# Order sums of a polynomial attention layer as accumulating transfers, and a reordered vector queue

## The reference

```
h = _layernorm(x) * (1 + ca) + sa
x = x + ga * attn(h, W_in, W_out)
h = _layernorm(x) * (1 + cb) + sb
x = x + gb * ffn(h, ...)

# attn, per head of 16 channels
Tq, Tk = cheb(clip(q / 4)), cheb(clip(k / 4))
kv_beta = cumsum(Tk * v, axis=sequence) * beta
k_beta = cumsum(Tk.sum(channels), axis=sequence) * beta
num = (Tq * kv_beta).sum(orders)
den = (Tq.sum(channels) * k_beta).sum(orders)
out = (num / (den + 1e-7)) @ W_out.T

# ffn: top 2 of 8 experts, weight sqrt(softplus(logit)), plus the shared expert
y = shared(h) + sum_e combine[e] * (silu(h @ rW1[e] + rb1[e]) @ rW2[e] + rb2[e])
```

## Time and profile before

| | us |
|---|---|
| median of 3 runs (1147.56, 1149.32, 1340.12) | 1149.32 |
| the profiled execution's own time | 1148.21 |
| its span, first to last instruction | 1146.2 |

### The profile page before, as it was taken

One profiled execution on the slowest core, in us unless ns is written; L12 is line 12 of the kernel. 1 busy time (PEld: TensorE's weight loads), 2 busy tenths in 40 slices (PEclk: granted clock), 3 DMA queues, 4 the chain that ended last, 5 costly groups with the idle time before them and its releaser, 6 DMA issues.

```text
span 1146.2 us, 15452 instructions
## 1 busy us (share of the span) xinstructions
PE 968.0 (84%) x4889; PEld 689.4 (60%) x4889; DVE 962.7 (84%) x1465; ACT 521.1 (45%) x755; POOL 440.3 (38%) x606
## 2 busy tenths in 40 slices
PE   4865569898989899898989899898989899787997
PEld 3634255666757576666757476666757576555775
DVE  1499789989898998989898998989899898889542
ACT  4433344454536454454535455454635445342331
POOL 2044242443625254443525244443525243343220
PEclk9776779999999999999999999898989999888999
DMA  7100000000101010000101000010100000000000
GB/s 256 43 1 18 1 28 1 19 19 1 47 1 37 1 43 4 14 23 0 47 0 37 0 33 13 2 35 0 47 0 19 0 20 9 0 19 1 23 19 19
DMA packets 23069, 25.79 MB, mean 23 GB/s; under 512 B 1043, under 2 KB 21982, under 8 KB 23014
## 3 DMA queue, kind: packets, MB, share of 16 engines
q1 hardware_dynamic: 21410, 22.72, 6.1%
q10 hardware_dynamic: 1604, 2.46, 0.7%
HBM read 16.77 MB, written 8.40 MB: 22 GB/s over the span
## 4 chain that ended last, share of the span: by engine, by line
DVE 40%; PE 29%; issue 19%; POOL 4%; ACT 3%; DVEq 1%; POOLq 0%; ACTq 0%
PE ring L1256 14%; DVE feat L934 11%; PE acc L1390 11%; DVE feat L900 3%; DVE feat L902 3%; DVE hidL L1095 2%; DVE feat L957 2%; POOL feat L628 2%; DVE hid L1090 2%; DVE feat L891 2%; PE cfb L1364 1%; PE tr L1339 1%; DVE feat L992 1%; DVE feat L953 1%; DVE best L1065 1%
## 5 line engine op out<-in xcount | busy, mean ns | idle before, releaser
L765 ACT ACTIVATE hid<-ring,b1row 128x512 f32<-128x512 f32 x144 | 98.2, 686 | 175.4 <-PE ring L1256 175.1
L1390 PE MATMUL acc<-w,hid 128*128 128x256 f32 x640 | 155.4, 390 | 0.0
L1256 PE MATMUL ring<-n2H,w1H 128*128 128x512 f32 x288 | 106.1, 451 | 56.5 <-ACT feat L723 56.5
L1090 DVE TENSOR_TENSOR hid<-hid,cfb 128x512 f32<-128x512 f32 x128 | 86.6, 676 | 80.1 <-PE cfb L1364 79.7
L1390 PEld LDWEIGHTS acc<-w,hid 128*128 128x128 f32 x640 | 116.4, 190 | 27.9 <-issue 14.7
L636 POOL TENSOR_TENSOR best<-best,pool_c 128x8 f32<-128x8 f32 x16 | 27.1, 1693 | 257.2 <-DVE best L1071 257.2
L628 POOL TENSOR_TENSOR feat<-feat 128x1024 f32<-128x1024 f32 x32 | 96.6, 3036 | 9.2 <-DVE feat L953 6.9
L673 POOL TENSOR_TENSOR fin<-fin,x 128x512 f32<-128x512 f32 x32 | 52.9, 1673 | 117.0 <-DVE fin L1104 117.0
L934 DVE TENSOR_TENSOR_SCAN feat<-zero,carry,feat 128x512 f32<-128x512 f32 x80 | 97.1, 1265 | 0.0
L1256 PE MATMUL ring<-n2H,w1L 128*128 128x512 f32 x288 | 96.9, 419 | 0.0
L1256 PE MATMUL ring<-n2L,w1H 128*128 128x512 f32 x288 | 96.7, 419 | 0.0
(11 more groups left out here) (169 smaller groups left out, 2253.4 us busy)
## 6 DMA issues: line engine op xcount, KB each, us to landing
xin<-in_L_attn_x SPq DMA_DIRECT2D x16, 512.0 KB, 3.6
out<-fin SPq DMA_DIRECT2D x16, 512.0 KB, 2.9
gates<-gate_rows SPq DMA_DIRECT2D x16, 128.0 KB, 3.5
feat<-in_L_wmod SPq DMA_DIRECT2D x1, 1536.0 KB, 13.8
feat<-in_L_attn_W_in SPq DMA_DIRECT2D x1, 768.0 KB, 9.2
const<-in_constants ACTq DMA_DIRECT2D x1, 690.5 KB, 4.3
fin<-in_constants ACTq DMA_DIRECT2D x1, 512.0 KB, 5.4
w<-in_L_ffn_rW ACTq DMA_DIRECT2D x1, 512.0 KB, 8.9
```

The source lines that it names most:

```text
L765: a.activation(hid[:, e % NG], ring[bank][:, :], ACT.Silu, bias=b1row[:, e:e + 1]).then_inc(ring_copied, 1)
L1090: v.tensor_tensor(hid[:, e % NG], hid[:, e % NG], cfb[:, :], ALU.mult).then_inc(hidw_ready, 1)
L1256: last = mm(out, w, x, start=(n == 0), stop=(n == len(terms) - 1))
L1390: last = mm(acc[t // 2][:, t % 2], x[:, t * P:(t + 1) * P], w[:, e // 2], start=False, stop=(e == E), skip_group_check=True)
```

## The change

- Three of the four sums of the order products are now DMA transfers with an add, issued from POOL: orders 1 into 0, 3 into 4, then 4 into 0. DVE adds order 2 at the end. Two POOL instructions of 128x1024 and one of DVE go.
- DVE's calls are reordered: each `prefix` is followed soon by its product, order 2 is weighed and summed last, the statistics of chunk c+2 stand behind the third prefix sum, `odd` of the query stands behind the residual, and the carry is copied for each order apart.
- The gate `ga` is multiplied into W_out once per batch row on POOL (`scale_wo`), not into the projection's result on DVE.
- The residual x1 goes to the output by a plain store of SP, and the gated expert output is added to it in memory by a transfer from POOL, in place of two POOL additions and a store.
- The exponential of the routing is a power on POOL, not an activation on ACT.
- The tile `split` is half as wide, and three of its four transposes are smaller.

```diff
+        wo_g = sb("wo_g", [P, KD, D])
...
-            def store(i, p):
-                sp.wait_ge(fin_ready, 2 * number(i, p) + 2)
-                sp.dma_start(o_v[i, p], fin[:, :, :]).then_inc(stored[p], 16)
+            def store_x1(i, p):
+                sp.wait_ge(x1_ready, 2 * number(i, p) + 2)
+                sp.dma_start(o_v[i, p], x1[:, p]).then_inc(x1_stored[p], 16)
...
-            def add_orders(i, p):
+            def add_orders(i, p, n):
                 c = number(i, p)
-                for n in range(2):
+                if n < 2:
                     pool.wait_ge(products, ND * c + 2 * n + 2)
-                    g.tensor_tensor(f(W + 2 * n), f(W + 2 * n), f(W + 2 * n + 1), ALU.add).then_inc(added, 1)
+                else:
+                    pool.wait_ge(added[0], 16 * c + 16)
+                    pool.wait_ge(added[1], 16 * c + 16)
+                into, of = ((W, W + 1), (W + 4, W + 3), (W, W + 4))[n]
+                pool.sem_inc(sum_begun, 1)
+                g.dma_start(f(into), f(of), accum_op=ALU.add).then_inc(added[n], 16)
+
+            def exps(i, p):
+                c = number(i, p)
+                pool.wait_ge(log_parts, NLOG * c + 4)
+                ge(pool, soft_steps, NSOFT * c)
+                g.tensor_tensor(best[:, U].rearrange("p t k -> p (t k)"), k_("e", NT * K),
+                                best[:, NEG].rearrange("p t k -> p (t k)"), ALU.pow).then_inc(exp_ready, 1)
...
-            def add_residual(i, p):
-                c = number(i, p)
-                for h in range(2):
-                    pool.wait_ge(ffn_gated, 2 * c + h + 1)
-                    o = fin[:, 2 * h:2 * h + 2]
-                    g.tensor_tensor(o, o, x1[:, p, 2 * h:2 * h + 2], ALU.add).then_inc(fin_ready, 1)
+            def add_to_output(i, p):
+                pool.wait_ge(x1_stored[p], 16 * (i + 1))
+                pool.wait_ge(ffn_gated, 2 * number(i, p) + 2)
+                g.dma_start(o_v[i, p], fin[:, :, :], accum_op=ALU.add).then_inc(stored[p], 16)
+
+            def scale_wo(i):
+                pool.wait_ge(gate_loaded[0], 16 * (i + 1))
+                ge(pool, projected, 2 * number(i, 0))
+                ga = gates[:, 0:1].to_broadcast([P, KD, D])
+                g.tensor_tensor(wo_g[:, :, :], wo[:, :, :], ga, ALU.mult).then_inc(wo_ready, 1)
...
                 silu(5)
                 high(4)
                 copy("v0")
...
-            ORDERS = (0, 1, 3, 2, 4)
+            ORDERS = (0, 1, 3, 4, 2)
+            BY_WEIGHT = (0, 1, 3, 2)
...
             def finish_numerator(i, p):
                 dve.wait_ge(products, ND * c + ND)
-                dve.wait_ge(added, 2 * c + 1)
-                v.tensor_tensor(f(W), f(W), f(W + 4), ALU.add).then_inc(numerator, 1)
-                dve.wait_ge(numerator, 2 * c + 1)
-                dve.wait_ge(added, 2 * c + 2)
+                dve.wait_ge(added[2], 16 * c + 16)
                 v.tensor_tensor(f(W), f(W), f(W + 2), ALU.add).then_inc(numerator, 1)
...
             def residual(i, p):
-                dve.wait_ge(gate_loaded[0], 16 * (i + 1))
+                ge(dve, x1_stored[p], 16 * i)
                 for h in range(2):
                     dve.wait_ge(projected, 2 * c + h + 1)
-                    v.tensor_tensor(gated[:, h], tr[h][:, :].rearrange("p (t d) -> p t d", t=2), gate(0),
-                                    ALU.mult).then_inc(gated_ready, 1)
-                ge(dve, fin_ready, 2 * c - 2)
-                for h in range(2):
-                    dve.wait_ge(gated_ready, 2 * c + h + 1)
-                    v.tensor_tensor(x1[:, p, 2 * h:2 * h + 2], gated[:, h], xin_of(i, p)[:, 2 * h:2 * h + 2],
-                                    ALU.add).then_inc(x1_ready, 1)
+                    v.tensor_tensor(x1[:, p, 2 * h:2 * h + 2], tr[h][:, :].rearrange("p (t d) -> p t d", t=2),
+                                    xin_of(i, p)[:, 2 * h:2 * h + 2], ALU.add).then_inc(x1_ready, 1)
```

More of the change, by code:

```diff
@@ L3 @@
 from contextlib import ExitStack
+import math
 import numpy as np
@@ L111, in build @@
         tie = cv["tie"].unsqueeze(1).to_broadcast([P, NT, E * E])
-        PC = ("-half", "half", "one", "eps", "1/D")
+        PC = ("-half", "half", "one", "eps", "1/D", "e")
         pool_c = sb("pool_c", [P, len(PC)])
@@ L219, in build @@
         x_loaded = [sem(f"x_loaded{p}") for p in range(CB)]
+        x1_stored = [sem(f"x1_stored{p}") for p in range(CB)]
         stored = [sem(f"stored{p}") for p in range(CB)]
@@ L238, in build @@
         products = sem("order_products")
-        added = sem("orders_added")
+        added = [sem(f"orders_added{n}") for n in range(3)]
+        sum_begun = sem("order_sums_begun")
         numerator = sem("numerator")
@@ L431, in _ @@
                 for n, what in enumerate(PC):
-                    value = {"-half": -0.5, "half": 0.5, "one": 1.0, "eps": EPS_LN, "1/D": 1.0 / D}[what]
+                    value = {"-half": -0.5, "half": 0.5, "one": 1.0, "eps": EPS_LN, "1/D": 1.0 / D, "e": math.e}[what]
                     nc.gpsimd.memset(pool_c[:, n:n + 1], value).then_inc(s_pow, 1)
@@ L601, in _ @@
                 step(0, p, False, True)
-            with sp.Fori(1, B - 2) as i:
+            for p in range(CB):
+                step(1, p, True, True)
+            with sp.Fori(2, B - 2) as i:
                 for p in range(CB):
@@ L1120, in step @@
                     residual(*prev)
-                if second:
                     token_stats(dve, 1, *prev)
+                if attn_:
+                    odd(i, p, 1)
                 low(0)
@@ L1145, in step @@
                     prefix(i, p, 2)
-                if qkv:
-                    clip(*nxt, use, 0)
-                    clip(*nxt, use, 1)
+                if norm:
+                    token_stats(dve, 0, *after2)
+                if attn_:
+                    order_product(i, p, 2)
+                    prefix(i, p, 3)
+                expert(4)
+                if attn_:
+                    order_product(i, p, 3)
+                low(4)
                 if second:
@@ L1214, in _ @@
                 clip(0, 0, CHUNK0, q)
-            for q in range(2):
-                odd(0, 0, q)
+            odd(0, 0, 0)
             for i, p, st in FIRST:
@@ L1350, in combine_by_expert @@
                     pe.wait_ge(log_parts, NLOG * c + 1)
-                for t in range(NT):
-                    last = nc.tensor.transpose(misc[:, t * P:(t + 1) * P], split[:, t], ident)
+                nc.tensor.transpose(misc[:, 0:P], split[:, 0:2].rearrange("p t j -> p (t j)"), ident)
+                for t in range(1, NT):
+                    last = nc.tensor.transpose(misc[0:P // 2, t * P:(t + 1) * P], split[:, t], ident)
                 last.then_inc(split_T, 1)
```

118 lines of the change are left out of this document (55 added, 63 removed).

## The result

| | median us | of the kernel before |
|---|---|---|
| before | 1149.24 (4 runs) | 1 |
| after | 1179.16 (1178.51 to 1179.65, 4 runs) | 1.0265, 95% interval 1.0245 to 1.0285 |

The kernel got slower by 30 us. The profiled execution of the kernel after took 1179.41 us, with a span of 1177.7.

The account below looks back on a forecast made before the run. The prediction took a step as a ring paced by PE, DVE, then PE: 16.3 + 27.15 + 22.35 = 65.8 us against 64.7. Twelve steps add 13, the edges take 10: 1148.2 became 1151, range 1105 to 1190.

Parts of the forecast that it names:

- The chain: From DVE's late statistics over POOL's inverse roots, ACT and DVE to the v0 copy: sets the pace, 1137 to 1166, 0.55.
- the edges: Steps outside the twelve: two first -1.5 each, last first half -3, the one behind -3, last two -1; together -10.
- rival 2: Third transfer of the sums lands late, finish_numerator waits: each of 14 steps 3.2 us longer, total 1196; chance 0.12.
- Stretch A: Step start to the spread of expert 2, PE sets the pace: 16.6 us before, 16.3 after, transposes' 1.11 wait gone.
- Stretch B: Spread of expert 2 to the v0 copy and e6, DVE sets the pace: 23.9 us before, 27.15 after.
- term I: Time of POOL's inv_std for the first norm, between 4.9 and 7.3 us by the rows; taken as 6.1.
- Stretch C: From e6 to the next step's start, PE sets the pace: 23.6 us before, 22.35 after, two short waits gone.
- The sum: One step: 16.3 + 27.15 + 22.35 = 65.8 us against 64.7, +1.1; over twelve steps +13 us.
- The transfers: Accumulating transfers issued on POOL: 5.8 us landing and 1 us issue, 6.8 within 10.4 of slack, so no cost.
- Rival 3: POOL isn't freed, descriptors take as long as the additions, 3.04 us each; total stays 1151; included in the forecast's 0.55.
- Rival 1: Statistics don't limit, POOL hardly held, ACT early: step 63.0, total 1118, or 1099 without ACT's wait; chance 0.25.
- What would show it: Signs in the changed profile: steps 65 to 67 us, hidden_low idle 3 to 5, e6 gap 6 to 7, landing 5 to 8.

Follow-up runs that it names:

- e6: Not a run: expert 6 of the step, whose expert_up on PE waits for ACT's copy of v0.
- e4: Not a run: expert 4 of the step, whose hidden_low on DVE waits for its high part from ACT.
- the first experiment: Kernel after with one edit on DVE: the first norm's token statistics right behind the weighting of expert 2, ahead of the scans of prefix 1 and 2; 1154.98 us.
- two edits: On the kernel after with normalise_first late: last weighting of values ahead of hidden_low of expert 4, 1118.04 us; with the denominators' inverse ahead too, 1065.20 us.

## Why the prediction was right and wrong

The mechanism was right, its size was not: 1151 forecast, 1179 measured. The likeliest outcome named was no change that can be measured (0.47, against 0.26 for slower); it is 2.65% slower. The chain as I had summed it reached from 1137 to 1166 and a few us more for the edges, and 1179 lies above that. It lies inside the range of 1105 to 1190 only because the range had been widened upwards for rival 2, which did not occur; that part is luck. By the steps of the prediction, in the step from 567.87:

- **Stretch A**, 16.3 forecast. `weigh_hidden` of expert 2 starts at 584.12, 16.25 behind the start. The sum is right, its split is not: PE reached the spread after 14.96, earlier than the 15.5 that I took (16.6 - 1.1), and DVE started 1.3 behind it instead of 0.8 (the hand-over and the charge of 0.4 each), with its two scans at 4.5 us beside POOL's weighting. The wait at the transposes is gone, as forecast.
- **Stretch B**, 27.15 forecast, 29.46 measured (584.12 to 613.58). Here lies most of the miss, in the size of the terms and not in the chain: every link stands in the trace in the order that I gave. DVE up to the end of the statistics 12.0 (11.3): I had left out the small carry copies of 0.17 us that now follow each pair of scans in the step of a first half, and the start gap of 0.23 at 594.73. The term I, from there to ACT's start, 7.26 (6.1). ACT 3.20 (3.3). DVE from `hidden_low` to the end of the `weigh` 6.0 (5.7). From there to e6 0.97 (0.75).
- **The term I** is 1.16 of these 2.31 us. I took the middle of 4.9 and 7.3; the row to take was that of 7.3, since a product and scans stand back to back beside it in the new place. Four of its twelve instructions took 1.05 to 1.16 us in place of 0.2. That is 3.6 us of holds on the 3.3 of the unhindered twelve. With 7.3 in the sum, though, the forecast is 67.0 for a step, still 1.2 short of the measured 68.2.
- **Stretch C**, 22.35 forecast, 23.03 measured. The waits of 0.41 and 0.84 are gone. "PE is cold behind its gap as before, at no new cost" is the sentence that fell: PE waited twice, 8.9 us in all, and the clock behind was 0.50 where it had been 0.61. From e6 to the matmul of the head sums (613.58 to 619.30) PE took 5.7 us where it had taken 5.0 (590.50 to 595.50), and that is the 0.7 by which C is over.
- **The sum.** 68.74 in this step and 67.72 in the next, against 65.8. The excess of 2.4 us on average, twelve times, is 29 us, and the forecast lacked 28. The edges came to -11 for a forecast of -10, but term by term that is luck: the stretch ahead of the twelve steps is 3.6 us shorter (3 forecast), the two steps behind them 5.5 and 7.2 (3 each), and all that follows 5.1 us longer (1 shorter). Nearly all of the last is the end of the run: from DVE's last product to the last instruction, 5.4 us before and 9.9 now that a transfer that adds ends it. I had written "nothing either way" there.
- **The transfers**, 6.8 us for issue and landing forecast. Issue 0.92, landing 4.6. The third was issued at 616.89 and `finish_numerator` began at 628.45 without a wait: 11.6 us for 5.5. Rival 2 did not occur. Only in the two first steps, which have no experts, did `finish_numerator` wait for a transfer, 3.66 and 1.22 us, as the forecast had it. The Trainium skill, "DMA: Bandwidth & Descriptors", section "Anatomy of one DMA — SWDGE (gpsimd) path", gave 3.2 us by estimate; the trace has 4.6 for the transfers that add.
- **Rival 3**, POOL not freed, did not occur: an issue is 0.92 us of POOL, an addition 2.4 to 3.0. POOL's busy time in all stayed at 441 us even so, for it also has the exponential and `scale_wo` now.
- **Rival 1** did not occur in the kernel as it stands, but it priced what lies behind the chain: 1118 and 1099 in the prediction, and 1111 to 1115 in the runs that take the chain away. What the prediction held against it, the queue order on ACT, decided, and the runs on either end of the chain bear it out.
- **What would show it.** ACT's wait ended by POOL's `ms`, `hidden_low` of e4 with 5.01 us before it (3 to 5 forecast), no wait at the transposes: as forecast. Steps of 65 to 67: they are 68. One gap of 6 to 7 us at e6: they are two, 4.38 and 4.55. Landing in 5 to 8: it is 4.6.

I also missed on POOL's queue in the first experiment: the issue of a transfer is short, but the wait in front of it is not, and it holds whatever stands behind it on that engine.

## What to carry to other kernels

When an edit moves a producer, follow it to its consumer's queue and ask what stands behind the consumer there: here 30 us were lost with 56 us of DVE's work saved, and one call moved behind four others on ACT, busy for 40% of the span, gave 68 back. A transfer issued from a compute engine frees that engine only if what its issue waits for is early: here 10.3 us of wait stood ahead of an issue of 0.94, and putting the issue behind the work that others wait for gave 40 us. If a gap closes without gain, read where the next one opened before giving the edit up: of two edits the first lost 7 us alone, and the two together gained 46.

## What was not expected of the hardware

- POOL and DVE hold each other in both directions. The inverse roots' small instructions took 1.10, 1.12 and 1.16 us where 0.20 is usual, each ending with the DVE product or scan of 1.2 us beside it; a pair of DVE scans took 4.18 us in place of 2.33 beside a POOL addition of 2.39. The Trainium skill, "SBUF — State Buffer", section "Who interferes with whom", says that a DVE instruction with two SBUF inputs contends with a POOL instruction that reads SBUF. That whoever issues first has the port pair for the whole instruction, the section says of DVE's two-port modes; the prediction carried it over to the two-input case, and the rows above agree with it there too. The POOL instruction of 2.65 us in the earlier trace rows, and one of 2.83 in after, are longer than any one DVE instruction beside them, and that stays unexplained:

```profile
639.32 2.83 POOL L345 TENSOR_TENSOR ms<-stats 128x4 f32<-128x4 f32 x1 [2.86 <-DVE stats L374]
```

- An accumulating transfer of 512 KB within SBUF lands 4.6 us after its issue, 48 of them in a run, and in two steps of the loop the DMA share rose from 0.06 to 0.23. The loads of `xin`, 512 KB each and the same in both kernels, took 5.5 us where they had taken 3.6, and the 512 KB stores issued on SP 4.7 where those of the earlier trace rows took 2.9; that the added transfers are the cause is likely and not shown. In the loop no engine waited for either.
